# Experts of the edge layers in token halves, norms and projections by halves, routing by tanh: a four-layer network on one core

## The reference, cut to what matters

```python
x = x + tanh(g_xattn[0]) * scan_part(layernorm(x), ctx)             # q * scan(r = 0.9 r + ctx*ctx)
x = x + tanh(g_ffn[0])   * moe0(layernorm(x))                       # 8 experts, 128-512-128, gelu, top 2
x = x + tanh(g_xattn[1]) * attention(layernorm(x), ctx)             # 16 heads of 8, rope, biases
x = x + tanh(g_ffn[1])   * moe1(layernorm(x))                       # 8 experts, 352 hidden, silu(W1)*W3, top 2
x = x + tanh(g_xattn[2]) * pair_part(layernorm(x), ctx)             # tanh(text_t + feature_f) for all 64x64 pairs
x = x + tanh(g_ffn[2])   * moe2(layernorm(x))                       # 16 experts, 128 hidden, sigmoid, groups, top 4
x = x + tanh(g_xattn[3]) * attention(layernorm(x), ctx)
x = x + tanh(g_ffn[3])   * moe3(layernorm(x))                       # 8 routed experts and 1 shared, 512, gelu, + x

def layernorm(x): return (x - mean(x)) / sqrt(var(x) + 1e-5)
def moe0(x):                                                        # moe1 and moe3 likewise
    weights, indices = top_k(x @ gate_w.T + gate_b, 2); weights = softmax(weights)
    for e in range(8):
        w_e = sum(weights * (indices == e))
        out = out + w_e * (gelu(x @ w1[e] + b1[e]) @ w2[e] + b2[e])
def pair_part(features, text):
    h = tanh((text @ Ws)[:, None, :, :] + (features @ W)[:, :, None, :] + b)
    att = softmax(h @ w + mask); t = att @ text
    return tanh(t @ Wcw.T + bcw) * features + tanh(t @ Wcb.T + bcb)
```

## Time and profile before

| | |
|---|---|
| time, median of 3 runs | 670.05 us (666.01 to 670.86) |
| the profiled execution, its own time | 664.23 us |
| its span | 662.1 us |
| PE busy | 582.9 us, 88% |
| DVE busy | 467.8 us, 71% |
| ACT busy | 393.9 us, 60% |
| POOL busy | 116.0 us, 18% |
| chain that ended last, by engine | PE 67%, DVE 14%, ACT 11%, issue 3%, DMA 2%, POOL 2% |

### The profile page before, as it was taken

How to read it: one execution, slowest core, us unless ns; L and a number is a source line. 1 busy time by engine, 2 the same in 40 slices (tenths; PEclk the granted TensorE clock), 3 DMA queues, 4 the chain that set the end, 5 groups by cost and what they waited for, 6 DMA issues and landing times.

```text
span 662.1 us, 8458 instructions
## 1 busy us (share of the span) xinstructions
PE 582.9 (88%) x3205; PEld 393.4 (59%) x3211; DVE 467.8 (71%) x672; ACT 393.9 (60%) x501; POOL 116.0 (18%) x66
## 2 busy tenths in 40 slices
PE   5889999888898999998775558899997988999997
PEld 3458888656656777774121124656643665888885
DVE  4876878686636889886689653846766755678785
ACT  4278888534635566555989743433204654888884
POOL 6530000040010000003999500003104000000000
PEclk9999999986998999999899979999999899999999
DMA  6207010120001712020000000163412000621200
GB/s 225 63 21 273 33 64 0 68 68 2 2 1 25 265 35 68 0 64 25 9 2 0 1 0 0 33 241 125 145 34 96 2 2 0 217 104 33 64 0 32
DMA packets 15483, 40.40 MB, mean 61 GB/s; under 512 B 2218, under 2 KB 6570, under 8 KB 15444
## 3 DMA queue, kind: packets, MB, share of 16 engines
q1 hardware_dynamic: 15444, 39.88, 17.5%
HBM read 39.17 MB, written 0.70 MB: 60 GB/s over the span
## 4 chain that ended last, share of the span: by engine, by line
PE 67%; DVE 14%; ACT 11%; issue 3%; DMA 2%; POOL 2%; DVEq 0%; SPq 0%; ACTq 0%
PE ps L594 41%; ACT work L858 7%; PE ps L631 3%; PE ps L480 3%; PE ps L505 2%; PE ps L492 2%; PE ps L385 2%; PE ps L372 2%; PE ps L379 2%; DMA w_f<-in_w 2%; PE ps L608 2%; PE ps L610 1%; PE ps L609 1%; PE ps L571 1%; DVE diag L981 1%
## 5 line engine op out<-in xcount | busy, mean ns | idle before, releaser
L1270 DVE TENSOR_TENSOR h_lo<-h_act,h_hi 128x1024 fp32r<-128x1024 f32 (+2 forms) x116 | 115.9, 999 | 46.8 <-ACT h_hi L900 46.8
L594 PE MATMUL ps<-n_hi,w_hi 128*128 128x512 f32 (+1 forms) x232 | 81.7, 400 | 4.6 <-DVE h_act L1247 2.4
L1444 POOL TENSOR_TENSOR rstd<-var_eps,minus_half 128x4 f32<-128x4 f32 x16 | 16.8, 1057 | 378.4 <-DVE var_eps L977 378.4
L900 ACT CAST h_hi<-h_act 128x1024 fp32r<-128x1024 f32 x68 | 71.4, 1050 | 18.1 <-PE ps L594 16.4
L594 PE MATMUL ps<-n_hi,w_lo 128*128 128x512 f32 (+1 forms) x232 | 80.3, 394 | 0.0
L594 PE MATMUL ps<-n_lo,w_hi 128*128 128x512 f32 (+1 forms) x232 | 80.2, 393 | 0.0
L594 PE MATMUL ps<-h_hi,w_hi 128*128 128x512 f32 (+1 forms) x184 | 61.8, 394 | 5.5 <-DVE h_lo L1270 5.5
L858 ACT ACTIVATE work<-work,p_rest 128x2048 f32<-128x2048 f32 x32 | 61.3, 1990 | 8.6 <-DVE work L1151 8.4
L594 PE MATMUL ps<-h_hi,w_lo 128*128 128x512 f32 (+1 forms) x184 | 61.2, 391 | 0.0
L594 PE MATMUL ps<-h_lo,w_hi 128*128 128x512 f32 (+1 forms) x184 | 61.1, 390 | 0.0
L571 PE MATMUL ps<-work,p_rest 128*32 128x512 f32 x256 | 36.0, 641 | 26.0 <-ACT work L858 26.0
(11 more groups left out here) (221 smaller groups left out, 1063.2 us busy)
## 6 DMA issues: line engine op xcount, KB each, us to landing
work<-g_rows SPq DMA_DIRECT2D x38, 512.0 KB, 7.1
w_f<-in_w SPq DMA_DIRECT2D x17, 512.0 KB, 3.4
w_f<-in_w SPq DMA_DIRECT2D x8, 544.0 KB, 3.6
w_f<-in_w SPq DMA_DIRECT2D x16, 128.0 KB, 2.2
w_f<-in_w SPq DMA_DIRECT2D x16, 64.0 KB, 2.3
p_rest<-in_p_rest SPq DMA_DIRECT2D x1, 714.0 KB, 8.2
p_attn<-in_p_attn SPq DMA_DIRECT2D x1, 546.5 KB, 6.9
x<-in_xT SPq DMA_DIRECT2D x1, 512.0 KB, 3.5
```

What stands on the lines that cost most here:

```text
L594: mm = pe.matmul(dst[i], wap(wt, e, lo, size, rows), mv[i], start=(first and c == 0), stop=(last and c == 2))
L900: act.copy(h_hi[:, sl], h_act[:, sl]).then_inc(s["hi"], 1)
L1270: dve.tensor_tensor(h_lo[at_slot], src, h_hi[at_slot].bitcast(F32), ALU.subtract).then_inc(s["lo"], 1)
L1444: pool.tensor_tensor(rstd[:, r], var_eps[:, r], minus_half[:, r], ALU.pow).then_inc(ln["rstd"], 1)
```

## The change

It does six things.

- A list of orders per layer sets the steps. Layer 0's experts 0, 6 and 7, layer 3's expert 0 and its shared expert 8 take the token halves in turn (all chunks of half 0, then all of half 1; 6 and 7 together: half 0 of both, then half 1 of both); the others of these layers stay whole. Layer 1 takes the halves in turn in each expert, and 6 and 7 together at its end.
- Because half 0 of x is final before half 1's experts run, half 0's norm for the next layer is issued inside the flow of experts; the queries, scores, text and features that follow are issued by halves too. The finishing of an accumulator becomes finish(m, e, t).
- norm_diag and the product with ones are gone: PE multiplies rstd, broadcast along the columns, by the identity itself. A table LNBANK gives the banks.
- ACT computes tanh of half the difference, at step 3 of the experts, and DVE makes the exponential from it, (1 + e) / (1 - e), with three more instructions. In a layer's first steps DVE's routing is cut into pieces with a step's h_lo (and product) between. Gates are turned behind down step 5 and copied behind step 6.
- Work moves between stages: keys of attention 0 are copied by ACT at the start and rotated by DVE at steps 10 to 15 of layer 0's experts, and POOL expands them then; its values are copied by ACT; the weighted text and part of the text move into the pair sums; ACT's casts of the first weights of layers 1 and 3 move into pairs 2 to 5 of the attention, those of layer 2 behind the first features; POOL's four splits for layer 2 go to DVE in the pair sums. ACT loads tables by empty activations at chosen places.
- The warm-up operand is set by DVE, not by a DMA, and eight warm-up products stand ahead of the wait for x; eight stand behind the first scores of attention 1. In layer 2 the spread of gates by PE covers four half steps as before, but all 16 rows now come by DMA as well.

```diff
+    Moe(0, 8, 512, False, 2, 2, 2, [("halves", [0])] + [("whole", [e]) for e in range(1, 6)] + [("halves", [6, 7])]),
+    Moe(1, 8, 352, True, 2, 2, 3, [("halves", [e]) for e in range(6)] + [("halves", [6, 7])]),
+    Moe(2, 16, 128, True, 8, 4, 14, [("pieces", [e]) for e in range(16)]),
+    Moe(3, 9, 512, False, 2, 2, 2, [("halves", [0])] + [("whole", [e]) for e in range(1, 8)] + [("halves", [8])], routed=8),
...
             def norm_spread(j, t):
-                pe.wait_ge(ln["diag"], 2 * j + t + 1)
-                pe.matmul(ps[:, 4 + t], ones_w[:, :], diag[:, half(t)], start=True, stop=True).then_inc(ln["bc"], 1)
+                pe.wait_ge(ln["rstd"], 2 * j + t + 1)
...
+                    mm = pe.matmul(ps[:, LNBANK[j, t][2], i * P:(i + 1) * P], rstd[:, c:c + 1].broadcast_to([P, P]), ident, start=True, stop=True)
+                mm.then_inc(ln["bc"], 1)
...
+                if i == 0:
+                    pe.wait_ge(mo[0]["act"], MOES[0].total)
+                    queries(0)
+                    norm_mean(2, 1)
+                    norm_var(2, 1)
+                    scores(0)
+                    norm_spread(2, 1)
+                    scores(1)
+                    queries(1)
+                else:
+                    queries(0)
+                    queries(1)
+                    scores(0)
+                    scores(1)
+                    keep_busy(8, 4)
...
+            moe(MOES[0], {37: [lambda: norm_mean(2, 0)], 38: [lambda: norm_var(2, 0)], 41: [lambda: norm_spread(2, 0)]})
...
+            moe(MOES[1], {42: [lambda: norm_mean(4, 0)], 43: [lambda: norm_var(4, 0)], 44: [lambda: norm_spread(4, 0)], 46: [first_features]})
...
-                    act.activation(route_view("e", E), route_view("cur", E), ACT.Exp).then_inc(once["e"], 1)
+                        act.activation(route_view("e", E), route_view("cur", E), ACT.Tanh, scale=0.5).then_inc(once["e"], 1)
...
+                    if 2 <= p < 6:
+                        first_weights(MOES[(1, 3)[i]], p - 2)
                     if p == PAIRS - 1:
+                        load_table((ACT.Silu, ACT.Gelu)[i])
                         norm_square((3, 7)[i], 0)
...
+                query_rows(0)
                 if i == 0:
-                    prepare_values(0, 2)
-                    prepare_values(0, 3)
+                    norm_eps(2, 1)
                 soft(0)
+                if i == 0:
+                    norm_out(2, 1)
                 soft(1)
+                query_rows(1)
...
+                if L != 2:
+                    below = route_view("lg", E)
+                    link(dve.tensor_scalar(below, e, -1.0, 1.0, ALU.mult, ALU.add))
+                    link(dve.reciprocal(below, below))
+                    link(dve.scalar_tensor_tensor(e, e, 1.0, below, ALU.add, ALU.mult))
...
+            moe(MOES[0], {**keys, 17: [first_output], 18: [second_output], 19: [mask_bias],
+                          35: [lambda: finish(MOES[0], 6, 0)], 38: [lambda: finish(MOES[0], 7, 0)], 41: [lambda: norm_eps(2, 0)],
+                          42: [lambda: finish(MOES[0], 6, 1)], 43: [lambda: norm_out(2, 0), lambda: finish(MOES[0], 7, 1)]})
```

988 lines of the change are left out of this document (580 added, 408 removed).

## The result

The changed kernel takes 665.77 us (median of 20 runs, 663.06 to 667.96), the kernel before 670.64 us (20 runs, 662.05 to 672.78). The ratio is 0.9947, with a 95% interval of 0.9922 to 0.9971: faster by half a per cent, where 7% was forecast, and outside the range of 612 to 645. The profiled execution of before (664.23 us) is one in which the TensorE clock fell less than in most others of that kernel (mean granted clock 0.969, in most of the others 0.933 to 0.948), so it is 6 us faster than its median; the profiled one of after (667.81 us, clock 0.938) is near its own slow end. Between the two traces the span therefore grows, from 662.1 to 666.0.

The account below looks back on a forecast made before the run. Bound: expert products the change cannot remove, plus edges that are chains of small steps. Terms summed to 49.3 us saved, cut to 42 for handoffs and POOL's key expansion; 622 for the profiled execution, 625 after run spread, range 612 to 645.

Parts of the forecast that it names:

- The start, -11.7: Kernel start to layer 0's expert flow: shorter norm chains and halves starting apart make it 11.7 us earlier, bounds 6 and 13.
- Layer 0's edge, -10.9: Layer 0's end to attention 0's first turn: half the work overlaps or moves into the flow, 10.9 us less, bounds 6 and 12.
- layer 1's edge, -8.4: Layer 1's end to the first tanh: small groups move inside the flow, 8.4 us less, bounds 4 and 9.
- attention 0, -1.9: Attention 0, first turn to projection end: a busier PE keeps the clock higher, less 1.5 us for weight splits; 1.9 us less.
- Layer 0's flow (384 products at 0.226 us): Layer 0's expert products: price stays 0.226 us each, with 2 us allowed for POOL's key expansion now inside the flow.
- Attention 0's end to layer 1's flow, -5.6: Projection end to layer 1's expert flow: DVE sets the pace until step 5, gates turned; 5.6 us less, bounds 3 and 6.
- Pair sums, +1.0 (bounds 0 and 6): Stage of 32 tanh: ACT sets it, DVE stays ahead except at sum 30; 1.0 us more, bounds 0 and 6.
- Attention 1, +0.5: Attention 1: 1.5 us charged for weight splits, 1 us given back by eight warm-up products; half a microsecond lost.
- the edges of layers 2 and 3, -2.4, -2.8 and -5.5: Behind the pair sums 2.4 us less, ahead of attention 1 2.8 less, ahead of layer 3's flow 5.5 less.
- The queues hold each other: Rival: engines' fixed orders delay PE's feeding steps, half of four large edge gains is lost, 15 us more, 640; chance 0.26.
- ACT is the bound: Rival: in the experts' half steps ACT takes 2.91 us against PE's 2.72, 3.8 us on 20 chunks, 629; chance 0.06.
- A flow at the lower clock: Rival: half steps make PE wait in layer 0's flow until it runs at 1.2 GHz, over 665 us; chance 0.02.

## Why the prediction was wrong, by its steps

- **The start, -11.7.** The first product came at 25.4, 9.5 us earlier and not 11.7, which is 2.3 of the miss. From 5.5 us on PE waits three times for POOL's power, 1.7 us in all, and is busy otherwise. A price was misread: the two records of 1.51 us in the earlier trace rows are one float32 product of 512 columns and not two, so 0.76 us is too little. In the trace of after one such product follows the other in 0.85 us (128.49 and 129.34), which on the eight of them ahead of the first expert product is 0.7 us. In kernels with the same start the first product came between 24.8 and 26.9, so up to 2 us differ from execution to execution; the rest of the miss was not traced to a term.
- **Layer 0's edge, -10.9; layer 1's edge, -8.4; attention 0, -1.9.** Right: 23.6 to 10.9 us, 12.3 to 2.3, 35.9 to 33.8. The steps that stood behind one another now run side by side, as the order rows suggested. For attention 0 there was luck in it: with the same instructions it took 32.5 to 37.1 us in the thirteen traces behind the change, with the clock between 1.00 and 0.84.
- **Layer 0's flow (384 products at 0.226 us).** Wrong by 9.3 us. The allowance of 2 us for POOL's expansion was mis-sized: its row was at hand (3.60 us for two n_lo that take 1.4 alone) and was applied to one pair of passes, not to 9.73 us of expansion in a row. Spacing the expansions gave back 3.0 us and the later copy of the gates 2.7, both together 5.6; the other 3.7 us were not traced to one cause.
- **Attention 0's end to layer 1's flow, -5.6.** The step that failed is "then DVE sets the pace [...] until step 5; gates turned". It walked DVE and PE through the routing but not ACT's queue, in which the copy stands behind step 6 and holds whatever comes later. It cost 5.8 of the 9.4 us lost in layer 1 (some 3 the wait, 2.7 the half clock behind it), and 2.1 to 2.7 in layers 0 and 3.
- **Pair sums, +1.0 (bounds 0 and 6).** This is the largest error, 20.8 measured. The step that failed is "walked with its sums, it stays ahead of ACT except at sum 30". It took two things from rows without cover: the splits at their price alone, though POOL adds for all of this stage, and PE's products as if they were ready when DVE comes for them. DVE's work grew by 15 us where some 8 were counted, and 7.8 of it is the splits' price beside POOL (9.2 us, and 1.4 behind the last sum). Of the 20.8 us, reordering gives back 12.2 and the splits 7.9 by themselves, and 17.2 together; with the update of x moved as well the stage takes 68.4 us, less than the 70 forecast.
- **Attention 1, +0.5; the edges of layers 2 and 3, -2.4, -2.8 and -5.5.** The charge of 1.5 us for casts was too high (0.3 measured), yet attention 1 grew by 2.3 us: 2.0 of these lie behind the last pair's turn (7.8 us against 5.8), where a table load now stands and the projection runs at half clock (2.07 us against 1.21). In the kernel with the reordered pair sums, where the clock stayed up, that end took 6.5 us. Layer 2's edges lost to the clock what they gained: with it up, the stretch from its first product to the first turn took 104.1 us in one kernel, as walked (106.5 less 2.8), and 106 to 113 in those of 16 rows where it fell.
- **The rivals.** "The queues hold each other" is what happened, in a form that was not priced: it took no part of the edges' gains, but lost as much inside the stages. It had 0.26 and 640 us. "ACT is the bound" fell: where layer 0's experts 6 and 7 go by halves, the products lose about 1 us, and the one wait there is for a weight's low part, from DVE. "A flow at the lower clock" had 0.02, was looked for in the flow of layer 0 only, and came in the pair sums and layer 2. By the Trainium skill, "TensorE: Matmul & The Clock Gate", section "What's actually happening", activity releases the higher clock; the prediction used that for an edge that got busier and did not ask which stages would get less busy. The trace of after agrees with the rule there: 0.79 in the pair sums, where PE waits, against 0.96.
- **The tell-tales** named the right thing: waits of PE for DVE in layer 1's flow of more than 3 us (4.2 measured) and pair sums that grow by more than 3 us were two of the three signs of a wrong forecast, and both showed.

What remains open: how much of the 7 us that the reordered pair sums gave behind them is the clock, and what decides where the clock falls. The edge ahead of attention 0 has the same instructions in thirteen traces, and its clock is 1.00 in five and 0.85 in eight (10.9 and 11.3 us). The mean clock differs from run to run too (0.938 to 0.950 in one kernel), and single traces cannot separate this from an edit.
